# A graph kernel on one core: the edge convolution's sums in four column tiles

## The reference

```
xn  = layernorm(x)
msg = relu(xn[src] + edge_attr @ We + be)          # the edge convolution
z   = xn + segment_sum(msg, dst, 6250)
x   = x + layernorm(relu(relu(z @ W1 + b1) @ W2 + b2) + xn) * gamma + beta + mixer(xn)
x   = x + experts(layernorm(x))     # gates from attention over a second list of 131072 edges
```

## Time and profile before

| | us |
|---|---|
| runs shown, median of 3 | 2954.41 (2949.12 to 2954.65) |
| the profiled execution, its own time | 2958.44 |
| its span, first to last instruction | 2956.7 |
| TensorE busy | 2220.6 |
| VectorE busy | 1543.3 |
| GpSimd busy | 1730.4 |

### The profile page before, as it was taken

The page is one execution under the profiler, slowest core; times in us unless marked ns, Lnnn a source line. Parts: engine busy times, 40 slices in busy tenths (PEclk is TensorE's granted clock), DMA queues, the critical chain, the costliest instruction groups (busy, mean ns, idle before and its releaser), DMA issues. The chain is left out here.

```text
span 2956.7 us, 32307 instructions
## 1 busy us (share of the span) xinstructions
PE 2220.6 (75%) x10560; PEld 1599.5 (54%) x10560; DVE 1543.3 (52%) x2958; ACT 764.0 (26%) x1254; POOL 1730.4 (59%) x1689
## 2 busy tenths in 40 slices
PE   2578888899999899999979679999999990000018
PEld 2355677666766666666647546666666660000006
DVE  7778566556556655565547634433333340003984
ACT  1223343233333233332324411111111110000015
POOL 2444566456656556665525367777777777775411
PEclk9688999999999999999989789999999995555559
DMA  6744456543434343433333242222222221112627
GB/s 206 246 141 123 128 149 198 196 115 115 127 116 121 114 117 113 120 113 91 96 108 113 67 102 59 54 53 53 53 52 53 53 60 17 16 17 53 217 69 321
DMA packets 273390, 320.67 MB, mean 108 GB/s; under 512 B 98529, under 2 KB 228022, under 8 KB 272216
## 3 DMA queue, kind: packets, MB, share of 16 engines
q0 software_dynamic: 68416, 133.35, 18.4%
q1 hardware_dynamic: 160280, 144.68, 16.0%
q10 hardware_dynamic: 44544, 40.69, 4.4%
HBM read 241.24 MB, written 77.32 MB: 108 GB/s over the span
## 5 line engine op out<-in xcount | busy, mean ns | idle before, releaser
L744 POOL DMA_INDIRECT c_xg<-xb_dram,src x784 | 805.9, 1028 | 560.8 <-PE ps_a L783 329.6
L2160 POOL DMA_INDIRECT er<-row_dram,gi x784 | 741.1, 945 | 240.5 <-issue 219.8
L2556 PE MATMUL ps_c<-eo,shift 128*128 128x256 f32 x294 | 68.6, 391 | 442.6 <-ACT shift L2520 438.3
L783 PE MATMUL ps_a<-c_xg,c_inwin 128*128 128x256 f32 x1568 | 391.6, 395 | 2.5 <-ACT c_xg L952 2.5
L2215 PE MATMUL ps_em<-zT_all,ew 128*128 128x512 f32 (+1 forms) x832 | 352.8, 577 | 23.8 <-DMA eb_r<-in_eb 23.5
L2234 PE MATMUL ps_en<-ew,hid 128*128 128x256 f32 x1568 | 347.0, 379 | 0.6 <-DVE deg L2350 0.6
L783 PEld LDWEIGHTS ps_a<-c_xg,c_inwin 128*128 128x128 f32 x1568 | 300.0, 197 | 81.7 <-issue 42.4
L2234 PEld LDWEIGHTS ps_en<-ew,hid 128*128 128x128 f32 x1568 | 297.9, 190 | 60.7 <-issue 23.2
L771 PE MATMUL ps_e<-c_we,c_eaT 64*128 64x256 f32 x1568 | 236.5, 422 | 115.7 <-DVE c_xg L1100 110.8
L2556 PEld LDWEIGHTS ps_c<-eo,shift 128*128 128x128 f32 x294 | 56.3, 195 | 454.6 <-issue 447.1
L2280 ACT ACTIVATE hid<-ps_em,eb 128x512 f32<-128x512 f32 (+1 forms) x208 | 137.4, 662 | 569.8 <-PE ps_em L2215 569.5
(11 more groups left out here) (292 smaller groups left out, 2801.7 us busy)
## 6 DMA issues: line engine op xcount, KB each, us to landing
c_eaT<-in_eaT SPq DMA_DIRECT2D x196, 128.0 KB
eo_dram<-eo ACTq DMA_DIRECT2D x48, 512.0 KB, 3.0
eo<-eo_dram SPq DMA_DIRECT2D x8, 2048.0 KB, 11.3
c_xg<-xb_dram,src POOLq DMA_INDIRECT x784
er<-row_dram,gi POOLq DMA_INDIRECT x784
c_xl<-xn_dram SPq DMA_DIRECT2D x24, 512.0 KB, 4.8
c_xm<-xm_dram SPq DMA_DIRECT2D x24, 512.0 KB, 4.4
erow<-c_none ACTq DMA_DIRECT2D x1, 10240.0 KB, 45.3
```

What stands on the lines that cost most here:

```text
L744: pool.indirect_dma_start(xg[:, k % NB, b, :], None, M["xb_dram"], bass.IndirectOffsetOnAxis(ap=M["src1"][:, k * B + b:k * B + b + 1], axi ...
L783: t = pe.matmul(ps_a[:, k % 2, 0:D], inwin[:, k % 2, b, :], xg[:, k % NB, b, :], start=(b == 0), stop=(b == B - 1), skip_group_check=True)
L2160: pool.indirect_dma_start(er[:, r, b, :], None, M["row_dram"], bass.IndirectOffsetOnAxis(ap=gi[:, r, b:b + 1], axis=0)).then_inc(s_get[r], 16)
```

## The change

Each step's 1024 edges become four quarters of 256 edges (2 blocks), and each quarter has a window of its own, of 32 nodes instead of 128 and with its own first destination. A quarter's sums are made in one of four column tiles of the array: stationary operand 128 x 32, output to 32 partitions of ps_a. The 8 matmuls of a step go through the four tiles in turn, twice, and each tile's last one signals s_am. add_up(k, 0) is gone; all 8 matmuls stand where add_up(k, 1) stood and wait for both halves of the messages. inwin shrinks to a quarter. add_window becomes four adds of 32 nodes each, and every one waits until the one before has ended (s_agg), since windows can overlap. The transposes and ScalarE's copy stay as they were.

```diff
+NWIN = 4
+WIN = P // NWIN
+WB = B // NWIN
...
-        inwin = sb("inwin", [W1E, 2, B, P])
+        inwin = sb("inwin", [W1E, 2, B, WIN])
...
-                        pool.wait_ge(s_am, k - NB + 1)
+                        pool.wait_ge(s_am, NWIN * (k - NB + 1))
...
-                def add_up(k, x):
-
-                    if x == 0:
-                        pe.wait_ge(s_win, k + 1)
-                        if k >= 2:
-                            pe.wait_ge(s_agg, k - 1)
-                    pe.wait_ge(s_msg, 2 * k + x + 1)
-                    for b in range(x * HB, x * HB + HB):
-                        t = pe.matmul(ps_a[:, k % 2, 0:D], inwin[:, k % 2, b, :], xg[:, k % NB, b, :], start=(b == 0), stop=(b == B - 1), skip_group_check=True)
-                    if x == 1:
-                        t.then_inc(s_am, 1)
+                def add_up(k):
+
+                    pe.wait_ge(s_win, k + 1)
+                    if k >= 2:
+                        pe.wait_ge(s_agg, NWIN * (k - 1))
+                    pe.wait_ge(s_msg, 2 * k + 2)
+                    for j in range(WB):
+                        for w in range(NWIN):
+                            b = w * WB + j
+                            t = pe.matmul(ps_a[w * WIN:(w + 1) * WIN, k % 2, 0:D], inwin[:, k % 2, b, :], xg[:, k % NB, b, :], start=(j == 0), stop=(j == WB - 1),
+                                          tile_position=(0, w * WIN), skip_group_check=True)
+                            if j == WB - 1:
+                                t.then_inc(s_am, 1)
...
                     units(k, 0)
-                    add_up(k, 0)
                     if k:
                         turn_sums(k - 1)
                     units(k, 1)
                     if k + 1 < S1:
                         project(k + 1, 1)
                     units(k, 2)
-                    add_up(k, 1)
+                    add_up(k)
                     units(k, 3)
...
-                    act.wait_ge(s_am, k + 1)
+                    act.wait_ge(s_am, NWIN * (k + 1))
...
                     if k >= 2:
-                        dve.wait_ge(s_am, k - 1)
-                    nc.vector.tensor_tensor(inwin[:, k % 2, :, :], io[0:W1E, None, :].broadcast_to([W1E, B, P]),
-                                            rel[:, k * B:(k + 1) * B][:, :, None].broadcast_to([W1E, B, P]), ALU.is_equal).then_inc(s_win, 1)
+                        dve.wait_ge(s_am, NWIN * (k - 1))
+                    nc.vector.tensor_tensor(inwin[:, k % 2, :, :], io[0:W1E, None, 0:WIN].broadcast_to([W1E, B, WIN]),
+                                            rel[:, k * B:(k + 1) * B][:, :, None].broadcast_to([W1E, B, WIN]), ALU.is_equal).then_inc(s_win, 1)
...
                     dve.wait_ge(s_nt, k + 1)
-                    if k:
-                        dve.wait_ge(s_agg, k)
-                    at = nc.values_load(basei[0:1, k:k + 1], engines=[dve.engine], min_val=0, max_val=N - 1,
-                                        skip_runtime_bounds_check_because="VectorE clamped it to these bounds")
-                    here = M["zT"][:, :, bass.ds(at, P)]
-                    nc.vector.tensor_tensor(here, ps_a[:, k % 2, D:2 * D].rearrange("p (c n) -> p c n", c=KD), here, ALU.add).then_inc(s_agg, 1)
+                    sums = ps_a[:, k % 2, D:2 * D].rearrange("p (c n) -> p c n", c=KD)
+                    for w in range(NWIN):
+                        n = k * NWIN + w
+                        if n:
+                            dve.wait_ge(s_agg, n)
+                        at = nc.values_load(basei[0:1, n:n + 1], engines=[dve.engine], min_val=0, max_val=N,
+                                            skip_runtime_bounds_check_because="VectorE clamped it to these bounds")
+                        here = M["zT"][:, :, bass.ds(at, WIN)]
+                        nc.vector.tensor_tensor(here, sums[:, :, w * WIN:(w + 1) * WIN], here, ALU.add).then_inc(s_agg, 1)
```

More of the change, by code:

```diff
@@ L501, in conv_and_mixer @@
         we = sb("we", [2 * ED, D])
-        base = sb("base", [P, S1])
-        basei = sb("basei", [1, S1], I32)
+        base = sb("base", [P, S1 * NWIN])
+        basei = sb("basei", [1, S1 * NWIN], I32)
         rel = sb("rel", [W1E, S1 * B])
@@ L922, in _ @@
                 pe.wait_ge(s_pre, 1)
-                pe.matmul(ps_a[:, 0, 0:S1], first[:, :], M["dst1"][:, :].rearrange("e (s b) -> e s b", b=B)[:, :, 0], start=True, stop=True).then_inc(s_base, 1)
+                pe.matmul(ps_a[:, 0, 0:S1 * NWIN], first[:, :], M["dst1"][:, :].rearrange("e (m b) -> e m b", b=WB)[:, :, 0], start=True, stop=True).then_inc(s_base, 1)
                 pe.wait_ge(s_w, 32)
@@ L1066, in _ @@
                 dve.wait_ge(s_base, 1)
-                c.done(nc.vector.tensor_copy(base[:, :], ps_a[:, 0, 0:S1]))
+                c.done(nc.vector.tensor_copy(base[:, :], ps_a[:, 0, 0:S1 * NWIN]))
                 dve.wait_ge(s_const, 2)
@@ L1070, in _ @@
                 c.last()
-                c.done(nc.vector.tensor_scalar(basei[:, :], base[0:1, :], 0.0, float(N - 1), ALU.max, ALU.min))
-                c.done(nc.vector.tensor_tensor(rel[:, :].rearrange("e (s b) -> e s b", b=B), M["dst1"][:, :].rearrange("e (s b) -> e s b", b=B),
-                                               base[0:W1E, :, None].broadcast_to([W1E, S1, B]), ALU.subtract))
+                c.done(nc.vector.tensor_scalar(basei[:, :], base[0:1, :], 0.0, float(N), ALU.max, ALU.min))
+                c.done(nc.vector.tensor_tensor(rel[:, :].rearrange("e (m b) -> e m b", b=WB), M["dst1"][:, :].rearrange("e (m b) -> e m b", b=WB),
+                                               base[0:W1E, :, None].broadcast_to([W1E, S1 * NWIN, WB]), ALU.subtract))
                 c.last()
@@ L1087, in outside @@
                     c.last()
-                    c.done(nc.vector.scalar_tensor_tensor(near, rel[:, :], float(P), near, ALU.is_lt, ALU.mult))
+                    c.done(nc.vector.scalar_tensor_tensor(near, rel[:, :], float(WIN), near, ALU.is_lt, ALU.mult))
                     c.last()
@@ L1335, in _ @@
                 add_window(S1 - 1)
-                dve.wait_ge(s_agg, S1)
+                dve.wait_ge(s_agg, NWIN * S1)
                 dve.wait_ge(s_most, 1)
```

## The result

The changed kernel took 2928.23 us (median, 2923.71 to 2933.01) against 2954.41 before: ratio 0.992, 95% interval 0.990 to 0.994. It is 26 us faster, clear of the 6 us that a measurement tells from no change, where 62 were forecast. The profiled executions are 2958.44 and 2923.71 us, 35 apart.

A forecast was written before the change was run, and what follows sets the result against it. TensorE's work was taken to bound only the third part. Terms -156 + 62 + 20 + 16 - 4 = -62 us gave 2892 us on the median's scale, own range 2840 to 2935 (chance 0.47), wider range 2810 to 3010.

The forecast's parts named there:

- The sums at 0.86 us a step and mode changes of 0.4: TensorE, third part: sums fall from 3.46 to 0.86 us, array form changes add 0.4; 71 x 2.2 = -156 us.
- The chain on VectorE: Four dependent window adds hold VectorE 1.3 us longer a step: +62 us in the third part, +16 in the first.
- the factor 48: Third part: TensorE already waits for add_rows in 48 of 142 places, each passing on 1.3 us: +62 us.
- compare's cut: On VectorE, compare writes 256 elements instead of 1024: 0.8 us less a step.
- The second part, -4: Key-value part, 14 steps: about 1 us won in the 4 steps without sort work there, -4 us.
- The step that failed: Third part: TensorE reaches the second project 1.73 us earlier and waits for add_rows; 14 steps x 1.5 = +20 us.
- The clock: Granted clock, 0.97 in the last two parts and 0.87 in the first, may fall: nothing added, 20 us kept in the range.
- (b): TensorE's sums: only two tiles run at a time, sums take 1.73 us a step; 2958 us, chance 0.12.
- (c): TensorE's sums: the four tiles run one after another, so the sums keep 16 x 0.216 us; 3094 us, chance 0.17.
- (d): VectorE's windows: tiles work but register loads behind the wait take 0.8 us, a window 1.2; 3003 us, chance 0.08.
- (a): Third part: VectorE's delay is absorbed, only the 20 us is given back there; 2820 us, chance 0.16.
- The signs to look for: 16 sums records in about 1.3 us, L771's waits some 110 us (third part) and 55 (first), convolution end about 1430 us.

The follow-up runs named there:

- The chain alone: The kernel before with only its window add cut into four dependent adds of 32 nodes: 3091.82 us, ratio 1.048; in a later set 1.025.
- first chip: The chip of the first set of four experiments, on which the kernel before takes 2950.66 us.
- later sets: Runs of changed kernels on three other chips, where the kernel before takes 3325 to 3343 us; the changed kernel has ratio 0.985 there.
- one add: The changed kernel with one window add of 128 nodes a step instead of four, three of four places left out: 2798.17 us, ratio 0.948; later 0.962.
- two pairs of the later sets: Kernels differing by tiles alone: narrow compare without and with tiles and single add (0.995, 0.994; 0.962); four adds, wide compare, without and with tiles (1.025; 0.996).

## Why the prediction missed

Much was right: the direction, the four tiles side by side, and the chain on VectorE that gives most of the gain back. The size was wrong, by the steps of the prediction:

- The sums at 0.86 us a step and mode changes of 0.4, -184 + 28 = -156 us in the third part: TensorE's busy time there fell by 150. With each record counted until the next one starts, the sums fell by 194 us and the other work got longer by 44, by mode changes and the lower clock together. Right as a sum, partly by luck, since the prediction put nothing on the clock.
- The chain on VectorE, +62 in the third part and +16 in the first. A link is 0.70 us, as forecast, and a step's net hold 1.1 to 1.25 us instead of 1.3. But the factor 48 was misread; with 34 places 1.3 us make 44. The chain alone cost 89 us in the third part for 1.9 us, 66 of them waits and 23 longer work, so 1.1 us make 51. That the +62 comes so near is luck: too many places, and nothing for the clock. In time as a whole the chain costs 130 to 141 us for 1.9 us on the first chip, 68 to 74 for each, so 1.1 us make 75 to 81, against 78 forecast. This gives compare's cut the chain's own price. The later sets bear that out for a cut that is taken off the chain (about 45 us for each microsecond, as for the chain itself), not for one below VectorE's hold in the kernel before; on the first chip it was not run.
- The second part, -4: it came to +2. The step said that VectorE's later window would be absorbed; the chain costs 19 us there (183.9 against 165.0 with one add).
- **The step that failed** is the last of the third part: "now nearly all waits are at the first project, so I take 14 steps x 1.5 = +20". The 20 at the second project is right (18.8 us in 13 places). But it was taken for all that TensorE's earlier arrival turns into waiting, and the first project was counted only for what VectorE's delay adds. By the chain alone, 66 us of such waits for 1.9 us, a kernel whose VectorE is held 1.1 us longer waits 52 + 38 = 90 us at its first projects. The changed kernel waits 131, so the tiles themselves make 41 us there. The kernel with one add says the same, if that rate holds below VectorE's hold in the kernel before too: held 0.8 us less it should wait 52 - 28 = 24 us, and it waits 62. So the term was some 60 us (41 + 19) instead of 20. In idle time as a whole it is 66 us on the first chip (172.0 against 106 for the kernel before with 1.1 us of chain) and 62 and 70 in the two pairs of the later sets; how much of it lies at the first project differs between them. With it the tiles, forecast at 136 + 14 = 150 us, are worth 101 to 107 by difference on the first chip (26 + 75 to 81), and 3% in the later sets. So the third part went by -163 for TensorE's work (-156 forecast), +51 for the chain (+62) and +66 for the idle time that the tiles make (+20): -46 instead of -74. These 28 us are the miss; the second part's 6 and the first part's 8 the other way are small beside them. (The profiled executions are 35 us apart, the medians 26.)
- The clock, "I add nothing for it and keep 20 us in the range": it fell to 0.93. How much of the lengthened work is due to it is not separated from the mode changes; the chain-alone kernel, with TensorE's program unchanged, shows 23 us of longer work for 66 us of waits.

Rivals (b) and (c) fell with the four records in 0.42 us, (d) with links of 0.70 us, and (a) with waits that grew from 51 to 147 us. The signs to look for came out so: 16 records in 1.07 us (1.3 forecast), waits of 147 us in the third part (110) and 71 in the first (55), and an end of the convolution at 1456 us (1430).

Why the first project waits more is shown in part. TensorE holds back the products of units(k, 0) while it waits there for add_rows(k, 0), and VectorE waits for such products before its next add_rows. With the project behind those units TensorE's wait shrank by 38 us in the third part and 43 in the first, so its place matters. But VectorE's waits for the products L888 and L911 did not shrink with it, as a ring of waits would have it. Whether the rest is VectorE's own pace was not tried. Nor is it known why the chain costs half as much in the later sets.

## What to carry over

When one engine's work is cut, list every place where it already waits, and count part of the cut before each such place as lost (here some 60 of 160 us), and only then add what the other engine's delay brings; pricing one of two waits is not enough. Count such places by the matmuls' own waits, without those of the weight loads. A chain of small dependent instructions costs its links, not its busy time: load each one's address before its wait. In this kernel waits on TensorE also went with longer work behind them, so a wait removed can be worth more than its own length.

## What the runs showed of the hardware

- Four column tiles run the 16 float32 records of a step in 1.07 us (1.09 with both matmuls of a tile in a row). Four records one behind the other on one tile would take 3 x 0.216 + 0.38 = 1.03, and 16 on the full array took 3.62. Less the 0.16 us under the next record that is 0.91 against 3.46 us, 3.8 times the full array's rate. The estimate that the prediction worked out from the Trainium skill (TensorE: Matmul & The Clock Gate, Part 3), 3.2 times, would make it 1.1 + 0.16 = 1.26 us; the trace's 1.07 doesn't bear it out for these shapes.
- A register load on VectorE behind a fresh wait puts the next add 0.47 us after the end of the last; ahead of the wait, 0.24 us.
- A change of the window add on VectorE alone: the same TensorE program with 93 us more idle time over the whole convolution (1386.1 to 1516.9 us long, busy 1246.3 to 1283.8) is busy for 38 us more.
